# A small clear on GpSimd ahead of every group of four gathers, in a two-layer graph convolution on one core

## The reference

```python
norm = -dinv[src] * dinv[dst]                    # dinv = deg(src) ** -0.5
prop = lambda h: segment_sum(h[src] * norm[:, None], dst, N)
h = x @ W1_0 + prop(x) @ W1_1 + b1
h = layer_norm(h, gamma, beta)
h = where(h >= 0, h, 0.01 * h)
h = h @ W2_0 + prop(h) @ W2_1 + b2
out = layernorm(x + h)                           # no gamma or beta
```

## Time and profile before

| | us |
|---|---|
| time, median of 3 runs | 2687.54 (2678.63 to 2699.2) |
| the profiled execution's own time | 2690.22 |
| its span, first to last instruction | 2688.4 |
| gathers of layer 0, first to last issue | 143.5 to 1396.2 |
| gathers of layer 1, first to last issue | 1434.6 to 2656.1 |

### The profile page before, as it was taken

One profiled execution on the slowest core, in us unless ns is written; L12 is line 12 of the kernel. 1 busy time (PEld: TensorE's weight loads), 2 busy tenths in 40 slices (PEclk: granted clock), 3 DMA queues, 4 the chain that ended last, 5 costly groups with the idle time before them and its releaser, 6 DMA issues.

```text
span 2688.4 us, 28747 instructions
## 1 busy us (share of the span) xinstructions
PE 2063.3 (77%) x8006; PEld 979.2 (36%) x8006; DVE 978.1 (36%) x1503; ACT 415.2 (15%) x844; POOL 1609.5 (60%) x1721
## 2 busy tenths in 40 slices
PE   6448787878787887888875877777687878887886
PEld 6413333333333333334332333333333333333333
DVE  8953333333333333333322233233233333333333
ACT  4701111111111111112111000000000000000001
POOL 0466656556566666666654666666666666666663
PEclk9779898999898998889887988888898988888888
DMA  8676666666576676667755666666666676666674
GB/s 293 256 240 204 196 199 199 197 198 213 179 216 210 208 212 207 204 204 216 214 176 186 202 214 203 213 214 202 206 215 200 212 222 211 204 216 211 203 219 128
DMA packets 198930, 559.29 MB, mean 208 GB/s; under 512 B 33180, under 2 KB 33182, under 8 KB 198784
## 3 DMA queue, kind: packets, MB, share of 16 engines
q0 software_dynamic: 133120, 436.31, 54.9%
q10 hardware_dynamic: 44680, 81.73, 8.4%
q1 hardware_dynamic: 20984, 39.35, 4.0%
HBM read 493.08 MB, written 64.18 MB: 207 GB/s over the span
## 4 chain that ended last, share of the span: by engine, by line
another core or an unknown queue 33%; PE 29%; issue 18%; DVE 10%; ACT 5%; ACTq 2%; DMA 2%; DVEq 0%; POOL 0%; SPq 0%
PE bank L701 13%; PE bank L708 12%; DVE acc L1134 2%; PE bank L752 2%; DMA feat<-feat 2%; DVE onehot L1029 1%; ACT work L507 1%; ACT feat L517 1%; ACT work L496 1%; DVE work L1010 1%; DVE stats L1065 1%; PE bank L638 1%; DVE ring L888 1%; ACT std L501 1%
## 5 line engine op out<-in xcount | busy, mean ns | idle before, releaser
L397 POOL DMA_INDIRECT ring<-table,index x1664 | 1575.8, 947 | 940.6 <-issue 467.0
L701 PE MATMUL bank<-ring,onehot 128*128 x4096 | 1012.7, 403 | 177.1 <-SPq L361 87.1
L1134 DVE TENSOR_TENSOR acc<-acc,bank 128x512 f32 x512 | 351.3, 686 | 1622.7 <-remote 881.3
L701 PEld LDWEIGHTS bank<-ring,onehot 128*128 128x128 f16 x4096 | 420.8, 103 | 719.8 <-issue 340.4
L708 PE MATMUL bank<-wA,work 128*128 128x512 f32 x784 | 429.0, 698 | 174.3 <-ACT work L496 148.5
L708 PE MATMUL bank<-wB,base_in 128*128 128x512 f32 x784 | 378.9, 629 | 13.4 <-DVE acc L1100 8.1
L708 PEld LDWEIGHTS bank<-wA,work 128*128 128x128 f32 x784 | 171.8, 226 | 389.8 <-issue 215.2
L1029 DVE TENSOR_TENSOR onehot<-bank,rel 128x1024 f16<-128x1024 f32 x256 | 311.6, 1218 | 0.1
L752 PE MATMUL bank<-diag,acc 128*128 128x128 f32 x784 | 134.2, 323 | 144.3 <-DVE acc L1134 67.7
L708 PEld LDWEIGHTS bank<-wB,base_in 128*128 128x128 f32 x784 | 156.4, 205 | 180.5 <-issue 165.2
L496 ACT ACTIVATE work<-bank 128x512 f32<-128x512 f32 x98 | 58.5, 597 | 883.3 <-remote 616.5
(11 more groups left out here) (123 smaller groups left out, 724.3 us busy)
## 6 DMA issues: line engine op xcount, KB each, us to landing
ring<-table,index POOLq DMA_INDIRECT x1664
base_in<-feat ACTq DMA_DIRECT2D x98, 256.0 KB
feat<-feat SPq DMA_DIRECT2D x49, 256.0 KB, 3.1
table<-work SPq DMA_DIRECT2D x49, 256.0 KB, 2.9
feat<-feat ACTq DMA_DIRECT2D x49, 256.0 KB
table<-work ACTq DMA_DIRECT2D x49, 256.0 KB
feat<-in_x ACTq DMA_DIRECT2D x48, 256.0 KB
out<-work ACTq DMA_DIRECT2D x48, 256.0 KB
```

The costliest lines, as they stand in the source:

```text
L397: nc.gpsimd.indirect_dma_start(out=ring[:, at * ROW:(at + 1) * ROW], out_offset=None, in_=table[l], in_offset=bass.IndirectOffsetOnAxis(ap ...
L701: last = nc.tensor.matmul(bank[n % SUM_BANKS][:, :], hot, ring[:, bass.ds(slot_at + (2 * j + half) * D, D)], start=j + half == 0, stop=j + ...
L1134: nc.vector.tensor_tensor(acc_at, acc_at, bank[n % SUM_BANKS][:, :], ALU.add).then_inc(sums_added, 1)
```

## The change

Each group of four gathers gets one more GpSimd instruction ahead of it: a clear of 256 float32 in each of 128 partitions, in a block of its own (`pause`, two halves in turn) that nothing else reads or writes. It counts a semaphore of its own, `paused`, up by one, and waits on the same semaphore for the clear two groups before, which had written the same half. It stands behind the wait on `ring_free` and ahead of the gathers of the group. In all there are 416 such clears. Nothing is removed or moved.

```diff
+        pause = sb("pause", [P, 2, 2 * P], FP32)
...
+        paused = sem("paused")
...
                     wait(pool, ring_free, GROUPS * l + g - RING + 1)
+                    n = GROUPS * l + g
+                    wait(pool, paused, n - 1)
+                    nc.gpsimd.memset(pause[:, n % 2, :], 0.0).then_inc(paused, 1)
                     for j in range(GROUP):
                         at = k * GROUP + j
                         c = index_col(g * GROUP + j)
                         nc.gpsimd.indirect_dma_start(
```

## The result

The changed kernel takes 2703.94 us (median of 20 runs, 2689.56 to 2720.15). The kernel before took 2686.85 us beside it (20 runs, 2673.91 to 2699.2). The ratio is 1.0059 [1.0044, 1.0074], some 16 us. I had said 2827. The outcome is rival B: the clears are there, they cost GpSimd's queue something, and its waits took nearly all of it up.

A forecast was written before the change was run, and what follows sets the result against it. The prediction took GpSimd's gather issue to pace the kernel. 416 clears at 0.41 us made 171 us, less 34 absorbed in waits, so 137 on top of 2690.2 gave 2827 us, range 2600 to 2920.

The forecast's parts named there:

- rival B: GpSimd's waits for a free slot absorb the clears: 2690 to about 2715 us; chance 0.16 together with D.
- the two waits followed above: GpSimd's waits for a free slot at 1125.63 and 1941, read as GpSimd itself setting when they end.
- stop, drain and word: GpSimd halts at a full ring, gathers land, then TensorE's late step-done signal comes; claimed to shift together with GpSimd.
- the fifth that was let be absorbed: Share of the 171 us gross price expected to vanish in GpSimd's waits: 34 us, leaving 137.
- The size of the clear's price: GpSimd's queue: 0.41 us per clear, bounds 0.25 to 0.76, over 416 groups 171 us gross.
- The second wait: GpSimd's wait on `paused` for the clear two groups before: claimed to cost nothing in itself.
- the first gather behind a clear: GpSimd's gather after each clear: in the upper bound 1.10 us instead of 0.95.
- C: Dear pause: 0.76 us per clear on GpSimd, all on the path, 3006 us, or 2944 at 0.61; chance 0.13.
- Rival A: Pauses at GpSimd's groups let TensorE's late signals through: 2477 us if all waiting goes, 2669 if half; chance 0.26.
- near 210 us: Sign in the trace for rival B: what would be left of GpSimd's waits for a free slot.
- D: The clear runs beside the gather's 0.30 us gap and takes no GpSimd time: 2690 us; chance 0.16 together with rival B.
- the ceiling of 4.8 us: No GpSimd wait for a slot was longer; taken as fitting waits that end when gathers in flight land.

The follow-up runs named there:

- e3: The changed kernel with each clear at 1024 elements instead of 256: 2670.44 us beside 2682.79 unchanged; repeated, 2636.16 us beside 2308.47 unchanged.
- e2: The changed kernel with each clear at 512 elements instead of 256: 2699.97 us beside 2682.79 for the unchanged kernel, ratio 1.0054.
- f1_as_changed: The changed kernel run again to the letter: 2374.42 us beside 2308.47 for the unchanged kernel, ratio 1.0282.

## Why the prediction was wrong, step by step

**The step that failed** is "by the two waits followed above it does set it, and then stop, drain and word all move along", with the fifth that was let be absorbed. From waits that end when the DMA has drained I concluded that GpSimd's issue sets when the word comes. Measured, 56 to 61 of 77 us were absorbed with a clear of 256, 151 of 166 with 512, and all of 345 with 1024, there with some help of words that came earlier. A halt that ends with a drain shows that the two coincide, not that a later halt means a later end: the rows that I had the earlier trace rows would look the same if the words had come by something else and the gathers had been done by then. The simpler reading, which I had written down and set aside (the queue is taken for 84%, GpSimd has time to spare), gives rival B's time.

**The size of the clear's price** was the second miss. The 0.31 us of the clear were right (322 ns). The gap was not: I took 0.41 us, with 0.25 as a lower bound, and it is 0.19. The bound was wrong because I let the clear gain no more than the 0.06 us by which two clears overlap in the earlier trace rows, and took the 0.30 us behind a gather as lost. It isn't: 1112.75 stands right at the end of the gather that began at 1111.82. This miss alone would have left 2690 + 0.8 x 77 = 2752, with the first step still wrong; with the right absorption, even 0.41 gives 2705. So the first is the one that counts.

**The second wait** (`paused`) and **the first gather behind a clear**: right. It costs nothing (gather 0.95 us behind a clear; the one of 1.10 is again the program's first). C falls with it. The Trainium skill, GPSIMD Engine Reference, Instruction dispatch, states about 6 us for the first call of a freshly loaded kernel. Between clears and gathers in turn no run here shows it: the gather behind a clear takes 0.95 us.

**Rival A** is a real effect, but far from its point: the clears of 256 leave VectorE's waits on "remote" as they were. At 1.1 us between groups they fall by about a quarter (881 to 664 us), at 2.0 us they vanish. But by then the clears cost more than the words give back; the best of it, e3, is 0.5% under before in a late set and 14% over it in a prompt one.

**Rival B** was right in that the waiting absorbs the clears, in its time (2690 to 2715; measured 2704) and in its sign in the trace: waits for a slot shrink, and TensorE's waits for a group don't grow. Its condition, that the words come by TensorE's clockwork, is not shown: without gathers the walk takes 1963 us in a late set, and with half of them the words are prompt, so what times the words hangs on the gathers. Its "near 210 us" belonged to a gross price of 171; e2, which had that price, shows 232.5. I gave it 0.16 together with D, for which the ceiling of 4.8 us was too weak a ground: the changed kernel has waits of 6.3.

No kernel of these that computes the reference's result beats the one before in both kinds of sets, so it stays as it was.

## What to carry to other kernels

Price an instruction that is added to a queue of gathers from where its neighbour ends to where the next starts: what fits into the gap that the gather leaves anyway may be free. Read the chain on the page, too, before you call an engine the one that paces: here it had GpSimd at 0% before the change. Where an engine shows both "paces the rest" and "waits for the rest", don't settle it by following one wait; ask which of the sums stays constant as its load grows, and if there is one experiment to make, give it several doses (1, 512, 1024 and twice 1024 here), since a flat stretch and then a straight one tells cover from path. And run the unchanged kernel beside every variant: the same change was worth 0.6% in one set and 2.8% in another.

## What the hardware showed that I had not expected

One and the same program took 2685 us in some sets and 2310 in others (f1_as_changed 2374 as against 2704 of the recorded result), with the waits of VectorE named "remote" at 881 to 953 us in the one and none in the other. The changed kernel's mean granted clock of TensorE was 0.88 in its late set and 0.95 in its prompt one (f1_as_changed), with TensorE busy 76% and 81%; the stretch of 144 to 1200 us had a DMA share of 0.69 and 0.79. In the late sets the loss does not depend on the bytes gathered, is not there without gathers, and goes with half the gathers at an unchanged pace of GpSimd. A clear of float32 on GpSimd took 109 ns for 1 element a partition, 322 for 256, 537 for 512 and 969 for 1024, and a gather of 128 rows of half the length was as dear as one of whole rows (947 ns).
